# Attention block of a four-layer network: scores laid out as pairs of sequences, relative terms with the sequences innermost

## The reference, cut to what matters

```
xp = transpose(gn(x)).reshape(b*W, c, H)          # 512 sequences of length H = 128
q, k, v = split(bn(relu(w_qkv @ xp)))             # 8 heads; q, k: 4 channels; v: 8
qk = einsum('nhcp,nhci->nhpi', q, k)
qr = einsum('nhcp,cpi->nhpi', q, q_pos) * gate_qr  # q_pos[c, p, i] = pos[c, p - i + H - 1]
kr = einsum('nhcp,cpi->nhpi', k, k_pos) * gate_kr
att = softmax(sum of bn(qk, qr, kr) over the three, axis=-1)
att_v  = einsum('nhpi,nhci->nhcp', att, v * gate_v)
att_vp = einsum('nhpi,cpi->nhcp', att, v_pos * gate_v_pos)
```

## Time and profile before

| | |
|---|---|
| median of 3 runs | 19744.31 us (19741.57 to 19746.13) |
| profiled execution | 19778.58 us, span 19776.8 us |
| span of `split_qk` | about 1537 to 2212 us |
| span of `attention` | about 2217 to 6536 us, 64 blocks |
| PE, DVE, ACT, POOL busy over the span | 57%, 51%, 28%, 48% |
| mean granted TensorE clock | 0.688 of 2.4 GHz |

### The profile page before, as it was taken

The page is one execution under the profiler, slowest core; times in us unless marked ns, Lnnn a source line. Parts: engine busy times, 40 slices in busy tenths (PEclk is TensorE's granted clock), DMA queues, the critical chain, the costliest instruction groups (busy, mean ns, idle before and its releaser), DMA issues. The chain is left out here.

```text
span 19776.8 us, 195767 instructions
## 1 busy us (share of the span) xinstructions
PE 11295.5 (57%) x62482; PEld 5033.8 (25%) x62482; DVE 10181.0 (51%) x14908; ACT 5464.1 (28%) x7509; POOL 9546.2 (48%) x8283
## 2 busy tenths in 40 slices
PE   5553477777777103332333233333347899999998
PEld 2551244444444001111111111111112233333333
DVE  4557544444444333443444344344432577777777
ACT  1114333333333000000000000000000477777776
POOL 0113200000000106886888688688820477777777
PEclk9555565656656556666656666666679999999999
DMA  4004322222222494335333533533333202021211
GB/s 95 27 27 99 61 36 39 37 37 39 37 39 36 143 194 110 94 95 131 95 94 96 130 95 94 131 94 94 94 88 71 43 20 47 20 45 22 43 22 30
DMA packets 1429876, 1407.11 MB, mean 71 GB/s; under 512 B 777265, under 2 KB 1170753, under 8 KB 1413761
## 3 DMA queue, kind: packets, MB, share of 16 engines
q1 hardware_dynamic: 1137088, 743.01, 18.5%
q0 software_dynamic: 221184, 604.27, 10.6%
q10 hardware_dynamic: 70976, 50.83, 0.8%
HBM read 1036.88 MB, written 276.84 MB: 66 GB/s over the span
## 5 line engine op out<-in xcount | busy, mean ns | idle before, releaser
L1374 POOL DMA_INDIRECT dc_g<-corners,dc_idx x4608 | 5287.7, 1148 | 1325.8 <-issue 1255.1
L1990 POOL TENSOR_TENSOR df_sq<-df_sq 128x512 f32<-128x512 f32 x1920 | 2519.3, 1324 | 1944.7 <-ACT df_sq L1938 1898.9
L1447 PE MATMUL dc_ps<-ident,dc_s 128*128 128x128 f32 x2560 | 673.8, 429 | 4339.5 <-DVE dc_s L1538 4323.9
L2085 DVE SCALAR_TENSOR_TENSOR df_pr<-df_pk,vecs,df_h 128x512 f32<-128x512 f32 x2880 | 2093.8, 742 | 610.6 <-PE df_pk L1879 343.3
L1530 DVE TENSOR_TENSOR dc_g<-dc_g,dc_wt 128x2304 f32<-128x2304 f32 x512 | 1308.9, 2556 | 1795.5 <-DMA dc_g<-corners,dc_idx 1795.4
L1938 ACT ACTIVATE df_sq<-df_pk,vecs 128x512 f32<-128x512 f32 x2880 | 1935.3, 685 | 978.6 <-DVE df_pr L2085 955.0
L748 POOL TENSOR_TENSOR at_md<-at_mt,at_own 64x512 bf16<-64x512 f32 x256 | 267.6, 1045 | 4013.8 <-DVE at_mt L938 4013.8
L920 DVE SCALAR_TENSOR_TENSOR at_x<-at_pq,hconst,at_x 128x512 f32<-128x512 f32 x1024 | 741.3, 745 | 2191.3 <-PE at_pq L785 1657.6
L1407 ACT ACTIVATE dc_st<-dc_ps 128x512 f32<-128x512 f32 x640 | 327.1, 609 | 4735.9 <-PE dc_ps L1447 4728.1
L1447 PEld LDWEIGHTS dc_ps<-ident,dc_s 128*128 128x128 f32 x2560 | 471.6, 218 | 4523.5 <-DVE dc_s L1538 3145.9
L1876 PE MATMUL df_pk<-df_t,df_wp 64*128 64x512 f32 x3840 | 1351.1, 640 | 210.4 <-ACT df_sq L1938 156.7
(11 more groups left out here) (271 smaller groups left out, 17474.2 us busy)
## 6 DMA issues: line engine op xcount, KB each, us to landing
df_h<-df_h SPq DMA_DIRECT2D x160, 512.0 KB, 7.1
dc_g<-corners,dc_idx POOLq DMA_INDIRECT x4608
corners<-dc_xt SPq DMA_DIRECT2D x16, 4160.0 KB
at_a<-y SPq DMA_DIRECT2D x192, 192.0 KB
dc_xp<-x SPq DMA_DIRECT2D x8, 4096.0 KB
cv_xp<-x SPq DMA_DIRECT2D x8, 4096.0 KB, 52.5
y<-sp_p SPq DMA_DIRECT2D x128, 192.0 KB, 2.8
y<-sp_p SPq DMA_DIRECT2D x64, 384.0 KB, 4.3
```

The costliest lines, as they stand in the source:

```text
L1374: nc.gpsimd.indirect_dma_start(gt[:, r, k, :, :].rearrange("p a c -> p (a c)"), None, image, bass.IndirectOffsetOnAxis(ap=idx[:, s, r, k:k ...
L1447: i = nc.tensor.transpose(ps[:, j, 128 * r:128 * r + 128], sm[:, r % 2, 128 * j:128 * j + 128], env.ident[:, :])
L1990: nc.gpsimd.tensor_tensor(a, a, sq[:, (KK * n + other) % RING, :], ALU.add).then_inc(nadded, 1)
L2085: nc.vector.scalar_tensor_tensor(out=rows(pr[:, j % RING, :]), in0=rows(pk[:, j % BANKS, :]), scalar=env.vecs[:, bias:bias + 1], in1=shift ...
```

## The change

1. `split_qk`: for a = 1 the columns go to y2 as e (parity of the position), then position, then sequence. Rel's second half of rows is shifted by 1 instead of 64 to match, and `a` has the eight sequences innermost; `relative` r now makes positions 8r to 8r + 7, each matmul two neighbouring positions.
2. X is [32 pairs of sequences, 128 positions, 2]. `rel_to_x` writes whole stretches of it. `times_v` reads every second element, `times_vpos` reads 32 pairs.
3. VectorE's add of a bank becomes two operations of 256 elements, each of which reads two score columns of the bank in turn (the pair) and writes one stretch of X.
4. The transposed maxima go into ptt, which frees a bank; pvv has two banks.
5. `exp` is two operations of eight nh. The order on TensorE changes: V products in halves between the spreads, next scores directly behind the last spread, relative matmuls from unit one on (2, 5, 5, 4 in the four units in place of 0, 5, 5, 6), positional products on alternate banks.

```diff
-                                halves = lambda v: v.rearrange("c (w e h) -> c e w h", w=8, e=2) if a else v
-                                nc.vector.tensor_scalar(val[:, s, a, :].rearrange("c (e w h) -> c e w h", w=8, e=2) if a else val[:, s, a, :],
-                                                        halves(z[:, s, :]), env.ab[:, a:a + 1], env.ab[:, 2 + a:3 + a],
+                                from_z = z[:, s, :].rearrange("c (w h e) -> c e h w", w=8, e=2) if a else z[:, s, :]
+                                nc.vector.tensor_scalar(val[:, s, a, :].rearrange("c (e h w) -> c e h w", w=8, e=2) if a else val[:, s, a, :],
+                                                        from_z, env.ab[:, a:a + 1], env.ab[:, 2 + a:3 + a],
...
-        a = sb("at_a", [128, 2, 2, HEADS, NSEQ, H // 2], BF16)
+        a = sb("at_a", [128, 2, 2, HEADS, H // 2, NSEQ], BF16)
-        X = sb("at_x", [128, 2, NH, H])
+        X = sb("at_x", [128, 2, NH // 2, H, 2])
-        pq, ptt, prr, pvv, pss = pp("at_pq", 2), pp("at_pt", 2), pp("at_prr", 2), pp("at_pvv", 1), pp("at_ps", 1)
+        pq, ptt, prr, pvv = pp("at_pq", 2), pp("at_pt", 2), pp("at_prr", 2), pp("at_pvv", 2)
...
-                sp.dma_start(rel[48 + r0:48 + r1, H // 2:255], pb[r0:r1, t, 0:255 - H // 2]).then_inc(posd, 16)
+                sp.dma_start(rel[48 + r0:48 + r1, 1:255], pb[r0:r1, t, 0:254]).then_inc(posd, 16)
...
# transposed_maxima
-                    pe.wait_ge(mt_out, u)
-                nc.tensor.matmul(pss[0:64, 0, 0:128], mx[:, q % 2, :], env.ident[:, :], start=True, stop=True).then_inc(mt_done, 1)
+                    pe.wait_ge(subbed, 4 * u - 1)
+                nc.tensor.matmul(ptt[0:64, q % 2, 0:128], mx[:, q % 2, :], env.ident[:, :], start=True, stop=True).then_inc(mt_done, 1)
# spread
-                nc.tensor.matmul(ptt[:, t % 2, :], sel[:, t, :], ...
+                nc.tensor.matmul(ptt[:, (q + 1 + t) % 2, :], sel[:, t, :], ...
# times_v
-                    pe.wait_ge(exped, u + 1)
+                if t % 2 == 0:
+                    pe.wait_ge(exped, 2 * u + t // 2 + 1)
-                    last = nc.tensor.matmul(pvv[32 * j:32 * j + 9, 0, ...], vt[:, s, at:at + 9], X[:, s, nh, :], ...
+                    last = nc.tensor.matmul(pvv[32 * j:32 * j + 9, q % 2, ...], vt[:, s, at:at + 9], X[:, s, nh // 2, :, nh % 2], ...
# times_vpos
-                        last = nc.tensor.matmul(pvv[32 * j:32 * j + 8, 0, 64 * i:64 * i + 64], pv[:, :, 127 - p], X[:, s, :, p], ...
+                        last = nc.tensor.matmul(pvv[32 * j:32 * j + 8, bank, 64 * i:64 * i + 64], pv[:, :, 127 - p], X[:, s, :, p, :], ...
# relative
-                    p = 4 * r + i
+                    p = 8 * r + 2 * i
-                                            a[0:96, s, :, :, :, p].rearrange("c e h n -> c e (h n)"), start=True, stop=True)
+                                            a[0:96, s, :, :, p // 2, :].rearrange("c e h n -> c (e h) n"), start=True, stop=True)
...
-            RELS = {1: ((0, 1, 2), (3, 4)), 2: ((5, 6, 7), (8, 9)), 3: ((10, 11, 12), (13, 14, 15))}
+            RELS = {0: ((0, 1),), 1: ((2, 3), (4, 5, 6)), 2: ((7,), (8, 9, 10, 11)), 3: ((12,), (13, 14, 15))}
+            def positional(k, s, f, bank, final):
+                if f < 2:
+                    free = lambda: pe.wait_ge(av_out, 4 * k + f + (3 if final else 2))
+                else:
+                    free = lambda: pe.wait_ge(vp_out, 4 * k + f - 1)
+                times_vpos(k, s, f, bank, free)
...
+                    spread_next(0)
+                    spread_next(1)
                     qk(k, s, q, (2, 3))
+                    times_v_next((0, 1))
+                    spread_next(2)
+                    times_v_next((2, 3))
+                    spread_next(3)
+                    if q < 3:
+                        qk(k, s, q + 1, (0, 1))
+                    elif not final:
+                        qk(k + 1, 1 - s, 0, (0, 1))
                     for part in range(2):
+                        if not final and part < len(RELS[q]):
+                            for r in RELS[q][part]:
+                                relative(k + 1, 1 - s, r)
                         if q == 0 and not first:
                             for f in (2 * part, 2 * part + 1):
+                                positional(k - 1, 1 - s, f, 1 - f % 2, False)
                         if part == 0:
                             transposed_maxima(k, s, q)
...
# VectorE
-                        nc.vector.scalar_tensor_tensor(out=x4(t), in0=pq[:, t % 2, :], scalar=env.hconst[:, h:h + 1], in1=x4(t),
-                                                       op0=ALU.add, op1=ALU.add).then_inc(added, 1)
+                        for i in range(2):
+                            x2 = X[:, s, 8 * q + 2 * t + i, :, :]
+                            last = nc.vector.scalar_tensor_tensor(
+                                out=x2, in0=pq[:, t % 2, 256 * i:256 * i + 256].rearrange("p (e b) -> p b e", e=2),
+                                scalar=env.hconst[:, h:h + 1], in1=x2, op0=ALU.add, op1=ALU.add)
+                        last.then_inc(added, 1)
...
# ScalarE: rel_to_x, exp
+                nc.scalar.activation(X[:, s, :, 8 * r:8 * r + 8, :], prr[:, r % 2, :].rearrange("p (q n e) -> p n q e", q=8, e=2),
+                                     ACT.Copy).then_inc(rel_out, 1)
+                for i in range(2):
+                    act.wait_ge(subbed, 16 * k + 4 * q + 2 * i + 2)
+                    g = X[:, s, 8 * q + 4 * i:8 * q + 4 * i + 4, :, :]
+                    nc.scalar.activation(g, g, ACT.Exp).then_inc(exped, 1)
-            RELS = {1: range(0, 5), 2: range(5, 10), 3: range(10, 16)}
+            RELS = {1: range(0, 5), 2: range(5, 11), 3: range(11, 16)}
```

More of the change, by code:

```diff
@@ L691, in load @@
                 whole = lambda y: y.rearrange("t (r h) f -> (t r) h f", h=HEADS)
[L692 removed]
+                halves = lambda y: y.rearrange("t (r h) (e p n) -> (t r) h e p n", h=HEADS, e=2, n=NSEQ)
                 for g, (r0, nt) in enumerate(GROUPS):
@@ L818, in times_v, with times_vpos @@
                     at = ((nh % NSEQ) * HEADS + nh // NSEQ) * 9
-                    last = nc.tensor.matmul(pvv[32 * j:32 * j + 9, 0, 128 * t:128 * t + 128], vt[:, s, at:at + 9],
-                                            X[:, s, nh, :], start=True, stop=True, tile_position=(0, 32 * j))
+                    last = nc.tensor.matmul(pvv[32 * j:32 * j + 9, q % 2, 128 * t:128 * t + 128], vt[:, s, at:at + 9],
+                                            X[:, s, nh // 2, :, nh % 2], start=True, stop=True, tile_position=(0, 32 * j))
                 if t == 3:
                     last.then_inc(av_done, 1)
-            def times_vpos(k, s, f, prev):
+            def times_vpos(k, s, f, bank, free):
                 if f == 0:
-                    pe.wait_ge(exped, 4 * k + 4)
-                    prev()
-                else:
-                    pe.wait_ge(vp_out, 4 * k + f)
+                    pe.wait_ge(exped, 8 * k + 8)
+                free()
                 for i in range(8):
@@ L833, in times_vpos @@
                         p = 32 * j + 8 * f + i
-                        last = nc.tensor.matmul(pvv[32 * j:32 * j + 8, 0, 64 * i:64 * i + 64], pv[:, :, 127 - p],
-                                                X[:, s, :, p], start=True, stop=True, tile_position=(0, 32 * j))
+                        last = nc.tensor.matmul(pvv[32 * j:32 * j + 8, bank, 64 * i:64 * i + 64], pv[:, :, 127 - p],
+                                                X[:, s, :, p, :], start=True, stop=True, tile_position=(0, 32 * j))
                 last.then_inc(vp_done, 1)
@@ L856, in work, with spread_next, times_v_next @@
                     older = (k, s, q - 2) if q >= 2 else (k - 1, 1 - s, q + 2)
-                    for t in range(2):
+                    def spread_next(t):
                         if not (first and q == 0):
                             spread(*prev, t)
-                    qk(k, s, q, (2, 3))
-                    for t in range(2, 4):
-                        if not (first and q == 0):
-                            spread(*prev, t)
-                    if not (first and q < 2):
-                        if q == 1:
-                            before = lambda: pe.wait_ge(vp_out, 4 * (k - 1) + 4)
-                        elif first and q == 2:
-                            before = lambda: None
-                        else:
-                            before = lambda: pe.wait_ge(av_out, 4 * k + q - 2)
-                        for t in range(4):
-                            times_v(*older, t, before)
+                    def times_v_next(ts):
+                        if first and q < 2:
+                            return
+                        if first:
+                            free = lambda: None
+                        elif q == 0:
+                            free = lambda: pe.wait_ge(av_out, 4 * k - 3)
+                        elif q == 3:
```

(14 more changed lines are left out.)

41 lines of the change are left out of this document (17 added, 24 removed).

## The result

| | before | after |
|---|---|---|
| median of runs | 19742.94 us, 4 runs | 19214.24 us, 4 runs (19206.5 to 19221.46) |
| ratio, 95% interval | | 0.9732 [0.9715, 0.9749] |
| profiled execution, its span | 19778.58, 19776.8 | 19221.46, 19219.7 |
| first to last spread of `attention` (L807) | 2289.6 to 6515.8: 4226.2 | 2287.3 to 5989.0: 3701.7 |
| placings (L748) between 2280 and 5500 us; so a block | 194; 4 x 3220 / 194 = 66.4 | 221; 58.3 |

The kernel is 2.7% faster; the forecast was 18965 with a range from 18740 to 19200, so the time came out 249 us above the forecast and 14 above the range. Of the 557 us between the two profiled executions 524.5 lie between the first and the last spread.

What follows compares the result with a forecast made beforehand. Bound by a loop of TensorE's work plus its stalls, no engine full. Saving 12.55 us a block over 63 intervals, 790 us less 8, gave 18997 from 19778.6; with the runs' median 34 lower, 18965 us, range 18740 to 19200.

Steps and rivals of the forecast that it cites:

- The step that failed: Loads for unit one's first relative matmuls: last issue 14 us into unit four, wanted at 22, leaving 8 us to land.
- rival 5: Stalls return elsewhere: each unit's waits for ScalarE's first copy (1.65 us) and for maxima (1.85) are new; priced in.
- Relative matmul 0.107: TensorE's relative matmuls, with eight sequences side by side, fall from 0.217 to 0.107 us each, 7.0 us a block.
- Rival 2: Relative matmuls stay at 0.216 us because weights or the two-level pattern bind, not the step: 19250 us; chance 0.12.
- Positional f 1.83: Positional matmuls in unit one: reading pairs takes a group from 0.145 to 0.107 us, one f from 2.42 to 1.83.
- Rival 1: Pairs don't help the positional reads: group 0.145 us, f 2.42, kernel 19110 us; chance 0.17.
- V products at no loss: Products with V on TensorE read every second element and lose nothing; upper bound double.
- Two adds in 0.80: VectorE's add of a bank, split into halves reading PSUM in 512-byte steps, takes 2 x (0.267 + 0.13) = 0.80 us.
- rival 4: VectorE reads pairs from PSUM slowly, 2.7 us per add: 20215 us; chance 0.04 with anything else slower.
- The walk: TensorE's work plus stalls re-added in the new order: units 16.17, 12.27, 12.39, 15.25 us; block 56.1, less 1.3: 54.8.
- Split stage: Before the attention: the turned half of L586 takes 0.34 us more, 0 to 11 us in all, taken as 8.
- Rival 3: TensorE's clock stays at 2.4 GHz as it stands less: block 51.4 us, kernel 18750 us; chance 0.14.

Runs made afterwards that it cites:

- early: Changed kernel with the six relative-operand loads on their own semaphore, issued once the last block's relatives are done; 18969.72 us, ratio 0.9611.
- first: Changed kernel with loads issued when they were, but the six relative-operand ones ahead of the nine others, with their own semaphore; 18977.52 us, ratio 0.9613.
- back: Changed kernel with no relative matmuls in unit one, put back into units two to four, loads untouched; 18960.02 us, ratio 0.9608.
- rel16: early with the relative matmuls reading their 128 columns 16 bytes apart (other relative terms computed); 19260.99 us, ratio 0.974.
- pad: combine with rows of X 1088 bytes long instead of 1024, the reference still computed; 18870.23 us, ratio 0.9498.
- rot: combine with each column tile's position turned by its number, rows of X unchanged (output positions permuted); 18868.53 us, ratio 0.9491.
- pad_only: Changed kernel itself with rows of X 1088 bytes long instead of 1024, nothing else; 19098.23 us, ratio 0.9675.
- combine: early with VectorE, in unit one, combining the last unit's maxima ahead of its first add instead of behind it; 18899.84 us, ratio 0.956.
- vp_apart: early with the positional matmuls reading 64 single elements 512 bytes apart instead of 32 pairs (other products); 19398.28 us, ratio 0.9811.

## Why the prediction came out as it did

The direction and the gain from the new layout and order were right, the time was 249 us too low, and one step carries the miss.

**The step that failed.** "The last is issued at 4060.43, 14 us into unit four ... the first relatives of unit one come 22 us behind that S, which leaves 8 us to land." The prediction let this stand as enough and put the wait for the loads at nothing. After has the last issue 13.8 us behind that S, and the relatives are wanted at 4026.11 - 4.94 = 4021.17, 21.7 behind it: both terms held to 0.3 us. What was never priced is the landing, for which the step had no row at all. It takes 12.2 us, and early, first and back show what that cost: 54.6 against 58.3 a block, 245 us of time (18969.72 against 19214.24). On their own chip's runs of before, the ratios 0.9732 and 0.9611 say the same. It is a new stall, and rival 5, under which new stalls were said to be priced in, listed only those for ScalarE and the maxima. The trace of before had the number. Windows of before behind the last issue, which ended at 4061.09:

```profile
4061.10:4067.00 5.90, 2.65 (x14) 1.09 (x11) 2.09 (x4) 1.03 (x2) 1.04 (x1) 0.50 0.30 44
4067.00:4072.00 5.00, 3.03 (x34) 1.30 (x34) 4.90 (x9) 0.33 (x1) 0.00 (x0) 0.50 0.22 52
4072.00:4077.00 5.00, 2.51 (x64) 2.16 (x64) 0.91 (x2) 2.21 (x3) 0.00 (x0) 0.55 0.00 1
```

The DMA share (the number before the last) is 0.30, 0.22 and then 0.00: the transfers ran on for some 11 us behind the last issue, and 8 could not do.

**The other steps.**
- Relative matmul 0.107: right. Four take 0.61 us in after, the mean is 307 ns. Rival 2 falls; in rel16, with the weights of after and a pattern of two levels too, the step alone brings the old price back. By the Trainium skill ("SBUF — State Buffer", Specifications) the cost is one of 16-byte lines hit only once; the trace agrees, 1.92 us for eight at 16 bytes as at 128.
- Positional f 1.83: the sum, 7.32 us, is what after shows (3.90 + 3.42), by two errors that cancel. Undisturbed f at 1.2 GHz take 3.61 / 2 = 1.81 us, but the second pair runs at 2.4 GHz, where 1.06 is possible (pad's 2.12) and the colliding addresses hold it at 1.71. Rival 1 falls. The rule of two hits in a line, as the prediction took it from the Trainium skill ("SBUF — State Buffer", Specifications), foresaw the full rate; the trace agrees only where the addresses don't collide (pad, rot).
- V products at no loss: right, 1.04 us for sixteen. Two adds in 0.80: right, 0.83 undisturbed, and the price of rival 4 is far off; but 2.18 and more beside the positional matmuls, which was not foreseen.
- The walk: unit three 12.39 against 12.23, four 15.25 against 14.72, two 12.27 against 10.82 (the fast clock reaches into it: 0.75), one 16.17 against 16.48 in early. With the 1.3 us taken off for the clock 54.8 against 54.6 in early. That this agrees to 0.2 us, and that early's 18969.72 lies 5 us from the 18965 forecast, is luck in part: the colliding addresses cost 1.8 to 1.9 us a block (pad_only, pad) that the walk had nowhere, and units two to four came out 2.1 us shorter than walked.
- Base block: 67.36 was one block; over the stretch the mean is 66.4, so the saving was taken 1 us a block, some 63 us, too high. It doesn't show in the total, since two things went the other way: the stretch outside the attention's spreads took 33 us less in after's profiled execution (15550.6 to 15518.0), part of it in stages that the change doesn't touch, and the split stage's 8 us can't be seen. No cause was found for the 33 us; the profiled execution of before was itself 34 us above its median, that of after 7, so they need not be the change's at all.
- Split stage: the turned half of L586 costs 0.50 us more instead of 0.34 (mean of both halves 1051 ns against 802, so 1300 for the turned one), and the first spread came at 2287.3 instead of 2289.6: hidden. Groups of after, 1536 to 2216 us:

```profile
L586 DVE TENSOR_SCALAR sp_v<-sp_z,ab 64x1024 f32<-64x1024 f32 x128 | 129.6, 1051 | 95.8 <-ACT sp_z L613 95.8
```

- Clock: 0.50 in units three and four as forecast. In unit two it rose from 0.60 to 0.75 (4019.16 to 4032.60 of before, 4034.59 to 4045.41 of after); no run tested why. The prediction had named a clock that moves in units two to four as a sign of being wrong. It took this unit at 1.2 GHz throughout and 1.3 us off the block for all such work. Rival 3 as a whole didn't come, but pad shows the part of it that the collisions ate (2.12 us instead of 3.55).

## What to carry to other kernels

When work is moved ahead, price the landing of its loads from the trace (issue of the last one to the end of the DMA share behind it), compare it with the time that the new order leaves, and put what is wanted first at the head of the queue with its own semaphore. When a layout changes, write down the byte distances at which parallel readers (rows, column tiles) walk, and look for neighbours on other engines whose mean duration grew: a row padded by 64 bytes gave back 0.6%. The best version, pad, has the early loads, the earlier combine and the padded rows, and takes 0.9498 [0.948, 0.9515] of the time before.

## What the runs showed of the hardware

- TensorE's reads can slow VectorE, ScalarE, GpSimd and TensorE itself by their addresses alone. With rows 1024 and tiles 256 bytes apart, two adds of 0.83 us took 2.62 (combine), four maxima reductions 4.49 instead of 2.48, a placing 2.07 instead of 1.04, an emptying on ScalarE 0.92 (after) instead of 0.60, and a positional group 0.111 us at 2.4 GHz instead of 0.066; with the rows at 1088 bytes, or the tiles turned, all of it was gone. The Trainium skill ("SBUF — State Buffer", SBUF: two separate sides) says that TensorE, ScalarE and VectorE's dedicated pair never wait on anyone; ScalarE's 0.92 and VectorE's 4.49 us show otherwise, and the measurement decides. Nor did the reductions wait for GpSimd: it stood idle for the 16.60 us up to 4015.34, and they ran from 4009.31 to 4013.80.
- Single elements 512 bytes apart took 0.145 us a group with the tiles 128 bytes apart (before) and 0.22 with them 256 apart (vp_apart).
- In after, fifteen loads issued one behind the other over 12 us (4001.65 to 4013.91) were in 12.2 us behind the last issue.
